# Memory attention of the first layer: second scores with keys on partitions, exponentials as the moving operand

## The chip, the cores and the metric

The kernel runs on one core of a Trainium2 chip. The metric is the device time of one execution in microseconds; the time before is the median of three runs. TensorE is called PE here, VectorE DVE, ScalarE ACT, GpSimd POOL and SyncE SP; PEld is PE's weight load.

## The reference, cut to what matters

The model has four layers with an attention part and a feed-forward part each, on h of 4 x 576 x 64 (64 patch tokens and 512 text tokens in each of 4 batches). The change touches one part, the feed-forward part of layer 0, a memory layer that ends in a causal attention over 8 heads:

```python
q = (x @ Wq).reshape(b, n, HEADS, DIM) * DIM ** (-0.5)      # b=4, n=576, HEADS=8, DIM=64
kv_scores, indices = _pk(x, Wq_pk, pk_keys)
ind = indices + offsets[None, None, :, None]
k = jnp.einsum('bnhk,bnhkd->bnhd', kv_scores, keys_table[ind])
v = jnp.einsum('bnhk,bnhkd->bnhd', kv_scores, values_table[ind])
sim = jnp.einsum('bihd,bjhd->bhij', q, k)
sim = jnp.where(causal, sim, neg)
attn = jax.nn.softmax(sim, axis=-1)
out = jnp.einsum('bhij,bjhd->bhid', attn, v)
out = out.transpose(0, 2, 1, 3).reshape(b, n, HEADS * DIM)
return out @ Wo
```

## The kernel before

The kernel is a row of stages; each opens its own semaphores and a block in which every engine runs its own instruction list, and the next block starts when all are through. `retrieval_stage` (L1508) first makes keys and values with `dense_rows_stage` and writes them to device memory as `kept`, one array of 128 rows (64 of key, 64 of value) by tokens for each head. Then comes the attention, which is what the change replaces. It has 32 heads in all (4 batches by 8 heads), unrolled, with the batch outside. n counts them.

A head has 576 tokens: chunks c = 0 to 4 of 128 queries (the last has 64), chunk c seeing keys 0 to 128(c+1). For each head, `RetrievedAttention` and its parent `CausalAttention` do this:

- SP fetches 128 x 576 of `kept` (L1025), two buffers.
- PE multiplies w_q by xnT to q, 64 x 576 (L1033), and transposes the value rows, five tiles (L1037). DVE copies q with the factor 0.125 (L1045) and v (L1049, L1051) out of PSUM. The same PSUM bank 0 is used in two turns, first q of 512 tokens, then the rest.
- `pe_score` (L811, L813): q chunk as weights, keys as the moving operand; the scores lie in PSUM with queries on partitions.
- `dve_head` (L913): one operation adds the mask, writes the scores to `probs` and takes the row maximum; L916 negates it. ACT takes the exponential with the maximum as bias and the sum as by-product (L881).
- `pe_turn_probs` (L823): 15 transposes of the exponentials to keys on partitions; ACT copies them to `pT` (L871, L874).
- `pe_weigh` (L1061): for chunk c, c+1 products with the turned exponentials (128 x 128) as weights and v (64 columns) as the moving operand.
- `dve_norm` (L893, L896): reciprocal of the row sums, one number for each query, at most 128 x 4; then the product into O.

The order on PE is written out by hand in `pe_head` (L846): the scores of chunks 2 to 4, the turns of q and v of the next head and the first two scores of the next head stand between the transposes and the products of this head. After each batch `project` (L1544, L1552) transposes O, ACT copies it, and PE multiplies by w_o; DVE adds to h (L1588).

All float32 products are written as one call and stand in the trace as two instructions. bfloat16 products and transposes stand as one.

Of the kernel before, what the change touches and what calls it, by code (L numbers as in the profile page):

```python
# [42 lines left out]
class Steps:  # L43
# [3 lines left out]
    def __init__(self, engine, semaphore):  # L47
        self.engine, self.semaphore, self.before, self.count = engine, semaphore, 0, 0
# [639 lines left out]
                nc.gpsimd.memset(ap, value)  # L688


class CausalAttention:


# [306 lines left out]
STRIPS = ((0, 1, 16), (1, 1, 8), (2, 1, 5), (3, 1, 4), (4, 1, 3), (5, 3, 2), (8, 8, 1))  # L1000
PAIRED = sum(n * w for _, n, w in STRIPS)
STRIP_AT = [sum(n * w for _, n, w in STRIPS[:i]) for i in range(len(STRIPS))]


class RetrievedAttention(CausalAttention):

    def __init__(self, nc, core, st, w_q, kept):  # L1010
        super().__init__(nc, core, st, D, 1.0, fetches=None)
        self.w_q, self.kept = w_q, kept
        self.kv = st.sb("kv", [P, 2, SEQ])
        self.kT = self.kv[:, :, :]
        self.qT = st.sb("qT_padded", [P, 2, SEQ])

    def begin(self):
        super().begin()
        set_stage(self.nc, "peer_q_padding", [(self.qT[D:P, :, :], 0.0)])

    def sp_fetch(self, sp, n):
        b, h = n // HEADS, n % HEADS
        if n >= 2:
            sp.wait_ge(self.scored, self.BEGIN + CH * (n - 1))
        sp.dma_start(self.kv[:, n % 2, :], self.kept[h, :, b * SEQ:(b + 1) * SEQ]).then_inc(self.fetched[n % 2], 16)  # L1025

    def pe_turn(self, pe, m, u, tail):
        nc, ps, n = self.nc, self.core.psum, 2 * m + u
        b, h = n // HEADS, n % HEADS
        pe.wait_ge(self.fetched[u], 16 * (m + 1))  # L1030
        pe.wait_ge(self.qk_copied, self.BEGIN + 4 * n + (1 if tail else 0))
        lo, hi = (BANK, SEQ) if tail else (0, BANK)
        last = nc.tensor.matmul(ps[0:D, 0, 0:hi - lo], self.w_q[:, h * D:(h + 1) * D],  # L1033
                                self.core.xnT[:, b * PAD + lo:b * PAD + hi], start=True, stop=True)
        if tail:
            for c in range(CH):
                last = nc.tensor.transpose(ps[0:self.rows[c], 0, (c + 1) * D:(c + 2) * D],  # L1037
                                           self.kv[D:P, u, c * P:c * P + self.rows[c]], self.core.ident[D:P, D:P])
        last.then_inc(self.turned, 1)

    def dve_turn(self, dve, n, u, tail):
        nc, ps = self.nc, self.core.psum
        lo, hi = (BANK, SEQ) if tail else (0, BANK)
        dve.wait_ge(self.turned, self.BEGIN + 2 * n + (2 if tail else 1))
        nc.vector.tensor_scalar(self.qT[0:D, u, lo:hi], ps[0:D, 0, 0:hi - lo], 0.125, None, ALU.mult  # L1045
                                ).then_inc(self.qk_copied, 1)
        if tail:
            dve.wait_ge(self.weighed, self.BEGIN + CH * (n - 1))
            nc.vector.tensor_copy(self.v1[:, u, 0:CH - 1, :], ps[:, 0, D:CH * D].rearrange("p (c d) -> p c d", d=D)  # L1049
                                  ).then_inc(self.qk_copied, 1)  # L1050
            nc.vector.tensor_copy(self.v1[0:TAIL, u, CH - 1, :], ps[0:TAIL, 0, CH * D:(CH + 1) * D]  # L1051
                                  ).then_inc(self.qk_copied, 1)

    def pe_weigh(self, pe, m, u, c):
        nc, ps, d, r, n = self.nc, self.core.psum, self.d, self.rows[c], 2 * m + u
        if c == 0:
            pe.wait_ge(self.normed, self.BEGIN + 2 * n)
        pe.wait_ge(self.p_copied, self.BEGIN + CH * n + c + 1)
        for m in range(c + 1):
            k = self.rows[m]  # L1060
            last = nc.tensor.matmul(ps[0:r, 1, c * d:(c + 1) * d], self.pT[0:k, self.pT_at[c] + m * r:self.pT_at[c] + (m + 1) * r],  # L1061
                                    self.v1[0:k, u, m, :], start=(m == 0), stop=(m == c))
        last.then_inc(self.weighed, 1)


def dense_rows_stage(nc, core, I, norm, kept):
# [438 lines left out]
LOG_AT = ONEHOTS_AT + 2 * HEADS + 2  # L1505


def retrieval_stage(nc, core, I, norm):  # L1508


# [2 lines left out]
    with Stage(nc, "peer") as st:  # L1513
# [3 lines left out]
        kept = nc.dram_tensor("peer_kept", (HEADS, P, TOKENS), F32, kind="Internal").ap()  # L1517
        dense_rows_stage(nc, core, I, norm, kept)
        loads.arrive()
        O = st.sb("O", [P, T, HEADS * D])  # L1520
        o1 = st.sb("o1", [P, 2, HEADS * D])
        set_stage(nc, "peer_padding", [(O[TAIL:P, CH - 1::CH, :], 0.0)])
        A = RetrievedAttention(nc, core, st, w_q, kept)
        A.begin()
        o_turned, o_copied, o_projected, o_added, vec = (
            st.sem(n) for n in ("o_turned", "o_copied", "o_projected", "o_added", "vector_steps"))
        ps = core.psum
        TERMS = HEADS * D // P
        out_of = lambda b, h: (lambda lo, hi, r: O[0:r, b * CH + lo:b * CH + hi, h * D:(h + 1) * D])
        with nc.Block() as block:  # L1530
            @block.sync
            def _(sp):
                for n in range(B * HEADS):
                    A.sp_fetch(sp, n)

            @block.tensor
            def _(pe):
                def project(b):
                    pe.wait_ge(A.normed, A.BEGIN + 2 * HEADS * (b + 1))
                    for t in range(b * CH, (b + 1) * CH):  # L1540
                        if t >= 2:
                            pe.wait_ge(o_copied, t - 1)
                        for k in range(TERMS):
                            last = nc.tensor.transpose(ps[:, 6 + t % 2, k * P:(k + 1) * P], O[:, t, k * P:(k + 1) * P],  # L1544
                                                       core.ident[:, :])
                        last.then_inc(o_turned, 1)
                        for done in ([t - 1] if t % CH else []) + ([t] if t % CH == CH - 1 else []):
                            pe.wait_ge(o_copied, done + 1)
                            if done >= 2:
                                pe.wait_ge(o_added, done - 1)  # L1550
                            for k in range(TERMS):
                                last = nc.tensor.matmul(ps[:, 4 + done % 2, 0:D], o1[:, done % 2, k * P:(k + 1) * P], w_o[:, k, :],  # L1552
                                                        start=(k == 0), stop=(k == TERMS - 1))
                            last.then_inc(o_projected, 1)
                    pe.wait_ge(o_added, (b + 1) * CH)

                for b in range(B):
                    A.pe_start(pe, b * PAIRS, 0)
                    if b:
                        project(b - 1)  # L1560
                    for h in range(HEADS):
                        A.pe_head(pe, b * PAIRS + h // 2, h % 2, h < HEADS - 1)
                project(B - 1)

            @block.scalar
            def _(act):
                def copy(b):
                    for t in range(b * CH, (b + 1) * CH):
                        act.wait_ge(o_turned, t + 1)
                        if t >= 2:  # L1570
                            act.wait_ge(o_projected, t - 1)
                        nc.scalar.activation(o1[:, t % 2, :], ps[:, 6 + t % 2, :], ACT.Copy).then_inc(o_copied, 1)

                for b in range(B):
                    if b:
                        copy(b - 1)
                    for h in range(HEADS):
                        A.act_head(act, b * HEADS + h, h % 2)
                copy(B - 1)

            @block.vector
            def _(dve):
                steps = Steps(dve, vec)

                def add(b):
                    for t in range(b * CH, (b + 1) * CH):
                        dve.wait_ge(o_projected, t + 1)
                        nc.vector.tensor_tensor(core.h[:, t, :], core.h[:, t, :], ps[:, 4 + t % 2, 0:D], ALU.add  # L1588
                                                ).then_inc(o_added, 1)

                for b in range(B):
                    A.dve_start(dve, b * HEADS, 0)
                    if b:
                        add(b - 1)
                    for h in range(HEADS):
                        A.dve_head(dve, steps, b * HEADS + h, h % 2, h < HEADS - 1, h > 0, out_of(b, h),
                                   out_of(b, h - 1) if h else None)
                add(B - 1)


CHANNELS = 3 * D
# [4 lines left out]
FREQ = SEQ + 1  # L1606
FCH = (FREQ + P - 1) // P
FREQ_ROWS = [min(P, FREQ - P * k) for k in range(FCH)]
TOKEN_ROWS = [min(P, SEQ - P * c) for c in range(CH)]


def root_stage(nc, core, name, x, sq, stat, scale, eps, ones=None):
# [1337 lines left out]
```

## Time and profile before

| what | value |
|---|---|
| time, median of 3 runs | 4470.99 us (4460.36 to 4479.04) |
| profiled execution, its own time | 4491.15 us |
| its span | 4489.0 us, granted clock 0.863 |
| PE busy | 3640.8 us (81%), 16965 instructions |
| PEld busy | 2172.9 us (48%) |
| DVE busy | 2651.9 us (59%) |
| ACT busy | 1496.4 us (33%) |
| POOL busy | 359.1 us (8%) |

The page divides the span into 40 slices of 112 us. The attention that is changed lies in the 20th to the 24th. "Idle before" is the time in which an engine stood still just ahead of the instructions of a group, with the releaser that ended most of it. A granted clock of 1.00 is 2.4 GHz, 0.50 is 1.2 GHz; a value between them is a mean over a stretch with both.

### The profile page before, as it was taken

To read this page: it belongs to the slowest core of one execution; us is meant where nothing else is said; L and a number is where in the kernel's file an instruction comes from. 1 tells how busy PE (TensorE), PEld (TensorE's weight loads), DVE (VectorE), ACT (ScalarE), POOL (GpSimd) and SP (SyncE) were. 2 spreads that over 40 slices of the span, in tenths; PEclk is the share of its full clock that TensorE was granted. 3 is DMA by queue.
4 is the path that set the end of the run, shared out by engine and by line. 5 is a ranking of instruction groups with operands and counts; after the bars stand their busy time and mean duration, and the time that the engine had idled before them with its cause. 6 is when DMAs were issued, how large, how long until landed. Compare 5 with 4: busy or idle time off the path is not lost. (4 is left out here: it accounts for less than half of the span.)

```text
span 4489.0 us, 57158 instructions
## 1 busy us (share of the span) xinstructions
PE 3640.8 (81%) x16965; PEld 2172.9 (48%) x17110; DVE 2651.9 (59%) x7758; ACT 1496.4 (33%) x2931; POOL 359.1 (8%) x351
## 2 busy tenths in 40 slices
PE   5528889999999999999799868848869372799867
PEld 4325545544454554444466645437747252344354
DVE  3369878777887877555333322144344555899812
ACT  2203444444444444444333330034432133100023
POOL 1000000000000000000000001111000000355500
PEclk8569999999999999999878877975579665899968
DMA  0102334443443444443000020000010002100000
GB/s 7 52 10 76 102 87 102 87 91 86 101 92 83 101 88 91 107 104 71 24 19 20 21 79 0 0 4 1 1 31 0 1 0 54 43 0 0 0 7 5
DMA packets 140950, 207.83 MB, mean 46 GB/s; under 512 B 35104, under 2 KB 119657, under 8 KB 135469
## 3 DMA queue, kind: packets, MB, share of 16 engines
q1 hardware_dynamic: 140717, 205.03, 19.1%
q8 instruction: 108, 1.77, 0.2%
q14 instruction: 125, 1.02, 0.1%
HBM read 115.66 MB, written 10.03 MB: 28 GB/s over the span
## 5 line engine op out<-in xcount | busy, mean ns | idle before, releaser
L1256 PE MATMUL psum<-pk_W,pk_kv 128*128 128x512 f32 (+1 forms) x2560 | 1203.8, 552 | 10.0 <-issue 9.8
L1487 DVE SCALAR_TENSOR_TENSOR pk_W<-psum,pk_E 128x512 f32<-128x512 f32 (+1 forms) x1280 | 810.5, 633 | 440.3 <-ACT pk_E L1354 407.2
L1354 ACT ACTIVATE pk_E<-psum 128x512 f32<-128x512 f32 (+1 forms) x1280 | 708.8, 554 | 1005.0 <-PE psum L1246 1003.1
L1256 PEld LDWEIGHTS psum<-pk_W,pk_kv 128*128 128x128 f32 x2560 | 465.4, 191 | 173.7 <-issue 27.0
L1245 PE MATMUL psum<-pk_stack,pk_spread 128*128 128x512 bf16 (+1 forms) x1171 | 420.4, 359 | 80.0 <-DVE pk_W L1487 53.6
L1246 PE MATMUL psum<-pk_stack,pk_spread 128*128 128x512 bf16 (+1 forms) x1280 | 459.4, 359 | 17.7 <-DMA pk_stack<-pk_marks 9.5
L2480 PE MATMUL psum<-tree_w,tree_x 128*128 128x512 bf16 x1692 | 381.0, 380 | 112.9 <-PEq L120 90.7
L1245 PEld LDWEIGHTS psum<-pk_stack,pk_spread 128*128 128x128 bf16 x1280 | 125.1, 98 | 444.8 <-DVE pk_W L1487 349.4
L2480 PEld LDWEIGHTS psum<-tree_w,tree_x 128*128 (+1 forms) x1728 | 168.2, 99 | 312.0 <-issue 121.3
L2551 DVE COPY_PREDICATED leaf_acc<-leaf_path,psum 128x512 f32<-128x512 uint32 x468 | 310.4, 729 | 5.1 <-PE psum L2480 2.8
L1246 PEld LDWEIGHTS psum<-pk_stack,pk_spread 128*128 128x128 bf16 x1280 | 125.7, 98 | 241.8 <-issue 232.0
L1220 PEld LDWEIGHTS psum<-pk_ranked,pk_onehot 128*128 128x128 bf16 x2304 | 168.3, 149 | 115.4 <-issue 102.8
L1220 PE MATMUL psum<-pk_ranked,pk_onehot 128*128 128x128 bf16 x2304 | 172.1, 230 | 56.9 <-DVE pk_onehot L1445 56.9
L1190 POOL TENSOR_TENSOR pk_parts<-pk_left,pk_parts 128x512 bf16<-128x512 f32 (+1 forms) x40 | 44.0, 1100 | 1814.9 <-ACT pk_parts L1325 1814.9
L1441 DVE TENSOR_TENSOR pk_onehot<-pk_idf,pk_count 128x2048 bf16<-128x2048 bf16 x144 | 175.4, 1218 | 1.2 <-PE psum L1220 0.6
L295 PE MATMUL psum<-ident,xn 128*64 128x128 f32 x160 | 34.2, 407 | 171.7 <-DVEq L269 157.6
L881 ACT ACTIVATE peer_probs<-peer_probs,peer_stat 128x128 f32<-128x128 f32 (+4 forms) x160 | 96.3, 602 | 222.9 <-DVE peer_stat L916 222.7
L811 PE MATMUL psum<-peer_kv,peer_qT_padded 128*128 128x128 f32 (+4 forms) x320 | 163.3, 603 | 5.9 <-DVE peer_v L1051 3.5
L913 DVE CUSTOM_DVE_ANT_0 peer_probs<-psum,peer_mask 128x128 f32<-128x128 f32 (+4 forms) x160 | 85.9, 537 | 116.2 <-PE psum L811 106.2
L1957 PE MATMUL psum<-moe_x,moe_w 128*85 x480 | 113.8, 388 | 43.6 <-PEq L120 42.3
L1061 PE MATMUL psum<-peer_v,peer_pT 128*128 128x64 f32 (+2 forms) x960 | 139.4, 289 | 0.0
L1061 PEld LDWEIGHTS psum<-peer_v,peer_pT 128*128 128x128 f32 (+2 forms) x960 | 123.7, 202 | 20.7 <-issue 15.3
(513 smaller groups left out, 4970.1 us busy)
## 6 DMA issues: line engine op xcount, KB each, us to landing
pk_kv<-in_kv SPq DMA_DIRECT2D x40, 2048.0 KB, 7.8
pk_stack<-pk_parts SPq DMA_DIRECT2D x768, 64.0 KB, 2.5
pk_stack<-pk_marks SPq DMA_DIRECT2D x256, 64.0 KB, 2.6
peer_kv<-peer_kept SPq DMA_DIRECT2D x32, 288.0 KB, 2.8
peer_kept<-pk_made SPq DMA_DIRECT2D x32, 256.0 KB, 2.1
tree_weights_x<-in_tree_w SPq DMA_DIRECT2D x32, 256.0 KB, 4.6
pk_stack<-pk_parts SPq DMA_DIRECT2D x192, 32.0 KB, 2.0
dft_cos<-in_cos SPq DMA_DIRECT2D x1, 2596.5 KB
```

The costliest lines, as they stand in the source:

```text
L811: last = nc.tensor.matmul(ps[0:r, bank, 0:min(w, BANK)], q, self.kT[:, u, 0:min(w, BANK)], start=True, stop=True)
L1061: last = nc.tensor.matmul(ps[0:r, 1, c * d:(c + 1) * d], self.pT[0:k, self.pT_at[c] + m * r:self.pT_at[c] + (m + 1) * r], self.v1[0:k, u, ...
L1220: last = nc.tensor.matmul(ps[:, 6 + h // 4, h % 4 * P:(h % 4 + 1) * P], onehot[:, h % 2, :, :, r], ranked[:, r, :], start=(r == 0), stop=( ...
L1245: nc.tensor.matmul(ps[:, n % 2, 0:N], spread[:, 1, c % 2, :], of, start=True, stop=True)
L1246: nc.tensor.matmul(ps[:, 2 + n % 2, 0:N], spread[:, 0, c % 2, :], of, start=True, stop=True).then_inc(x_made, 1)
L1256: nc.tensor.matmul(ps[:, 4, 0:N], kv[:, k % 2, c, :], W[:, n % 3, 0:N], start=(c == 0), stop=(c == CHUNKS - 1)).then_inc(acc_done, 1)
L1354: nc.scalar.activation(E[:, n % 2, 0:width(k)], ps[:, 2 + n % 2, 0:width(k)], ACT.Exp).then_inc(e_made, 1)
L1441: steps.do(nc.vector.tensor_tensor(onehot[:, h % 2, :, :, :], idf[:, :, h, :].unsqueeze(2).to_broadcast([P, 2, KEYS, TOP]), count64[:, :, ...
L1487: nc.vector.scalar_tensor_tensor(W[:, n % 3, 0:width(k)], ps[:, n % 2, 0:width(k)], TOP + 0.5, E[:, n % 2, 0:width(k)], ALU.is_gt, ALU.mul ...
L1957: last = nc.tensor.matmul(ps[0:HALF, 3 * which + u % 3, :], w[:, lo:lo + HALF], x[:, bass.ds(g * BANK, BANK)], start=(k == 0), stop=(k == 2))
L2480: last = nc.tensor.matmul(ps[:, n % BANKS, :], x[:, bass.ds(t * P, P)], w[:, c * BANK:(c + 1) * BANK], start=(k == 0), stop=(k == len(prod ...
L2551: ins = nc.vector.copy_predicated(acc[:, u, level + 1, :, :], over(mask.bitcast(U32), D), bank)
```

## The change

`RetrievedAttention` and the blocks that used it go; `memory_attention_stage` takes their place, one block for all 32 heads. The scores with queries on partitions are made as before, in the order of chunks 4, 3, 2, 1, 0, but serve only for the maxima (`peak`); the masked scores are written to a scratch tile and not read. The negated maxima are split into two bfloat16 pieces (`piece`), transposed on PE (`turn_peaks`) and copied to a 32-row tile (`copy_peaks`). The scores are made a second time with keys on partitions (`turned_scores`), and a bfloat16 product of a tile of ones with the pieces adds the negated maxima to them, another with the identity adds the mask. ACT's exponential of three full banks goes to `pT`, which is the moving operand of `weigh`; the weights are v (64 columns) beside 64 columns of ones, so that the output has the values on 64 partitions and the sums on the other 64, sides changing with the parity of the head. `norm` takes the reciprocal of the sums as they lie, 64 x 576, and multiplies. The output stays with the head's dimension on partitions (oT), so that `project` needs no transposes. ACT copies q (for two heads at once) and v out of PSUM, where DVE did.

```diff
+def turned_scores(bank_of, k, q, mask16, ident16, ones16=None, shift=None):
+    a, b, c = bank_of
+    def scores(to, keys, queries):
+        yield to, k[:, keys], q[:, queries], True, False
+        if shift is not None:
+            yield to, ones16[:, 0:to.shape[0]], shift[:, queries], False, False
+    def masked(to, at, n):
+        yield to, ident16[:, :], mask16[:, at:at + n], False, True
+    tri = lambda bank, at: masked(bank[:, at:at + P], LEAD, P)
+    return (
+        [*scores(a[:, :], slice(0, P), slice(LEAD, SEQ)), *masked(a[:, 0:P - LEAD], LEAD + LEAD, P - LEAD)],
+        [*scores(b[0:LEAD, 0:LEAD], slice(0, LEAD), slice(0, LEAD)), *scores(b[LEAD:P, 0:LEAD], slice(BANK, SEQ), slice(BANK, SEQ)),
+         *masked(b[:, 0:LEAD], 0, LEAD), *scores(b[:, LEAD:BANK], slice(P, 2 * P), slice(P, SEQ)), *tri(b, LEAD)],
+        [*scores(c[:, 0:SEQ - 2 * P], slice(2 * P, 3 * P), slice(2 * P, SEQ)), *tri(c, 0),
+         *scores(c[:, SEQ - 2 * P:BANK], slice(3 * P, 4 * P), slice(3 * P, SEQ)), *tri(c, SEQ - 2 * P)])
+def weighed_parts(v, p):
+    return ((slice(0, BANK), v[:, 0, :], p[:, 0, :]),
+            (slice(P - LEAD, BANK), v[:, 1, :], p[:, 1, LEAD:BANK]),
+            (slice(2 * P - LEAD, BANK), v[:, 2, :], p[:, 2, 0:SEQ - 2 * P]),
+            (slice(3 * P - LEAD, BANK), v[:, 3, :], p[:, 2, SEQ - 2 * P:BANK]),
+            (slice(4 * P - LEAD, BANK), v[LEAD:P, 4, :], p[LEAD:P, 1, 0:LEAD]))
...
+SCORE_ORDER = (4, 3, 2, 1, 0)
+SCORE_BANKS = (6, 6, 7, 6, 7)
+SCORE_FREE = (0, 1, 1, 2, 3)
...
+            @block.tensor
+            def _(pe):
...
+                def score(n, j):
...
+                    if n >= 1 or j >= 1:
+                        pe.wait_ge(peaked, CH * n + SCORE_FREE[j])
...
+                def weigh(n, some):
+                    parts = weighed_parts(v[:, n % 4, :, :], pT[:, n % 2, :, :])
+                    for i in some:
+                        pe.wait_ge(exped, 3 * n + (1, 2, 3, 3, 2)[i])
+                        if i == 0:
+                            pe.wait_ge(v_copied, 2 * (n + 1))
+                            if n:
+                                pe.wait_ge(normed, 2 * n)
+                        cols, lhsT, rhs = parts[i]
+                        last = nc.tensor.matmul(ps[:, 1, cols], lhsT, rhs, start=(i == 0), stop=(i == 4))
+                        if i == 4:
+                            pe.wait_ge(q_copied, 4 * min((n + 1) // 2 + 2, heads // 2))
+                            last = nc.tensor.matmul(ps[:, 2, 0:LEAD], v[0:LEAD, n % 4, 0, :], pT[0:LEAD, n % 2, 1, 0:LEAD],
+                                                    start=True, stop=True)
+                            last.then_inc(weighed, 1)
...
+                pe.wait_ge(pad_set, 6)
+                make_q(0)
...
+                for n in range(heads):
+                    more = n + 1 < heads
+                    if n:
+                        weigh(n - 1, (0,))
+                    if more:
+                        score(n + 1, 0)
+                    turn_peaks(n)
+                    if n:
+                        weigh(n - 1, (1,))
+                    if more:
+                        score(n + 1, 1)
+                        score(n + 1, 2)
+                    score_turned(n)
+                    if n % 2 == 0 and n + 2 < heads:
+                        make_q(n // 2 + 1)
+                    if n % HEADS == 3 and n >= HEADS:
+                        project(n // HEADS - 1, n + 2)
+                    if more:
+                        score(n + 1, 3)
+                    if n:
+                        weigh(n - 1, (2, 3, 4))
+                    if more:
+                        score(n + 1, 4)
+                    if n + 2 < heads:
...
+                        turn_v(n + 2)
+                weigh(heads - 1, (0, 1, 2, 3, 4))
+                project(B - 1, heads)
...
+            @block.vector
+            def _(dve):
...
+                def norm(n):
+                    b, h = divmod(n, HEADS)
+                    out, sums = side(n), other(n)
+                    to = oT[out, b % 2, h // 2, :]
+                    dve.wait_ge(weighed, n + 1)
...
+                    nc.vector.reciprocal(inverse[out, LEAD:SEQ], ps[sums, 1, :]).then_inc(inverted, 1)
+                    nc.vector.reciprocal(inverse[out, 0:LEAD], ps[sums, 2, 0:LEAD]).then_inc(inverted, 1)
+                    dve.wait_ge(inverted, 2 * (n + 1))
+                    nc.vector.tensor_tensor(to[:, LEAD:SEQ], ps[out, 1, :], inverse[out, LEAD:SEQ], ALU.mult).then_inc(normed, 1)
+                    nc.vector.tensor_tensor(to[:, 0:LEAD], ps[out, 2, 0:LEAD], inverse[out, 0:LEAD], ALU.mult).then_inc(normed, 1)
...
+                for n in range(heads):
+                    more = n + 1 < heads
+                    if more:
+                        peak(n + 1, 0)
+                    copy_peaks(n)
+                    if more:
+                        for j in range(1, CH):
+                            peak(n + 1, j)
+                        piece(n + 1)
+                    if n % HEADS == 3 and n >= HEADS:
+                        add(n // HEADS - 1)
+                    if n:
+                        norm(n - 1)
+                norm(heads - 1)
+                add(B - 1)
```

P is 128, SEQ 576, BANK 512, LEAD 64. The POOL list of the new block makes both masks (`causal_masks`: two memsets and five selects, one after the other) and then fills six tiles: ones16 (128 x 128), qT (128 x 2304), peaks (128 x 1152, bfloat16), pieces (128 x 320, bfloat16), v (128 x 2560) and oT (128 x 5120). PE waits for all of them. Before, POOL filled peer_O, the mask and the lower half of the q tile, in three blocks.

## Rows read from the trace of the kernel before

**Rows 1.** Windows: the attention, and all that follows it.
```profile
core 0: us, PE busy (x) PEld busy (x) DVE busy (x) ACT busy (x) POOL busy (x), PEclk, DMA share, GB/s
2145.39:2634.80 489.41, 433.43 (x2352) 295.04 (x2352) 179.84 (x756) 179.48 (x532) 5.05 (x4) 0.82 0.07 20
2634.80:4489.00 1854.20, 1339.84 (x6326) 878.67 (x6362) 938.87 (x1711) 440.03 (x795) 296.52 (x274) 0.77 0.05 13
```

**Rows 2.** Waits of PE, 2156 to 2640 us: engine line waited for, total, times, longest.
```profile
PE psum L823 <- ACT peer_probs L881: 34.1, 32, 1.2
PE psum L1033 <- DVE peer_qT_padded L1045: 3.5, 4, 0.9
```

**Rows 3.** Windows: stretches of the attention at either clock.
```profile
2179.00:2185.00 6.00, 4.95 (x28) 2.71 (x26) 3.50 (x12) 1.76 (x6) 0.00 (x0) 1.00 0.17 49
2185.50:2195.00 9.50, 9.50 (x39) 6.69 (x37) 1.51 (x8) 2.93 (x10) 0.00 (x0) 0.50 0.00 0
```

**Rows 4.** Timeline: start, us, engine line; float32 pairs at full clock, then eighteen small products.
```profile
2858.20 0.81 PE L1812 MATMUL psum<-dft_y,dft_isin 128*128 128x384 f32 x2
2858.84 0.81 PE L1812 MATMUL psum<-dft_y,dft_icos 128*128 128x384 f32 x2
...
2623.86 1.97 PE L1061 MATMUL psum<-peer_v,peer_pT 128*128 128x64 f32 x18
```

**Rows 5.** Timeline ahead of the attention: two bfloat16 and two float32 instructions a turn.
```profile
2132.85 0.10 PEld L1245 LDWEIGHTS psum<-pk_stack,pk_spread 128*128 128x128 bf16 x1 [0.24 <-DVE pk_W L1487]
...
2134.14 0.10 PEld L1245 LDWEIGHTS psum<-pk_stack,pk_spread 128*128 128x128 bf16 x1 [0.24 <-DVE pk_W L1487]
```

**Rows 6.** Lines by form, DVE: busy us, mean ns; three widths of reciprocal.
```profile
L2346 DVE RECIPROCAL sparse_soft_stat<-sparse_soft_stat 128x8 f32<-128x8 f32 x20 | 4.1, 203 | 0.7
L232 DVE RECIPROCAL norm_stat<-norm_stat 128x20 f32<-128x20 f32 x8 | 2.2, 278 | 2.3 <-ACT norm_stat L282 2.3
...
L580 DVE RECIPROCAL lin_stat<-lin_stat 128x40 f32<-128x40 f32 x1 | 0.4, 403 | 0.0
```

**Rows 7.** Lines by form: other operations out of PSUM, and a peak's readout.
```profile
L2238 DVE TENSOR_TENSOR sparse_kB<-psum,sparse_k_mask 64x512 f32<-64x512 f32 x4 | 2.7, 683 | 13.6 <-PE psum L2196 13.6
L896 DVE TENSOR_TENSOR peer_O<-psum,peer_stat 64x64 f32<-64x64 f32 x32 | 6.6, 205 | 0.0
L801 DVE COPY rot_soft_qT<-psum 96x512 bf16<-96x512 bf16 x16 | 6.7, 421 | 27.0 <-PE psum L785 27.0
L913 DVE CUSTOM_DVE_ANT_0 peer_probs<-psum,peer_mask 64x576 f32<-64x576 f32 x32 | 24.0, 750 | 4.6 <-PE psum L813 3.2 <-issue 0.4
L913 DVE CUSTOM_DVE_ANT_0 peer_probs<-psum,peer_mask 128x128 f32<-128x128 f32 x32 | 9.3, 292 | 2.4 <-PE psum L811 1.1
L913 DVE DVE_READ_ACCUMULATOR2_ANT peer_stat<- 128x1 f32 x128 | 10.2, 80 | 0.0
L1354 ACT ACTIVATE pk_E<-psum 128x512 f32<-128x512 f32 x1024 | 611.0, 597 | 820.5 <-PE psum L1246 820.4
```

**Rows 8.** PE timeline and windows around an idle stretch of PE.
```profile
2926.23 5.98 PE L315 MATMUL psum<-ident,tnn_uv 128*128 128x128 f32 x38 [5.12 <-PEq L155]
...
2911.00:2921.00 10.00, 10.00 (x32) 4.03 (x30) 0.55 (x1) 0.00 (x0) 0.00 (x0) 1.00 0.00 0
2926.50:2929.50 3.00, 3.00 (x16) 3.00 (x15) 0.69 (x1) 1.04 (x2) 0.00 (x0) 0.50 0.06 13
2929.50:2932.00 2.50, 2.50 (x24) 2.50 (x23) 1.78 (x3) 1.34 (x3) 0.00 (x0) 0.98 0.00 0
```

**Rows 9.** Timeline and lines of POOL's fills; the first product of the attention.
```profile
2145.39 1.80 POOL L688 MEMSET peer_O<- 64x2048 f32 x1 [76.75 <-POOLq L162]
2154.35 1.97 PE L1033 MATMUL psum<-xnT,peer_w_q 128*64 128x512 f32 x2 [14.03 <-DMA peer_kv<-peer_kept]
...
L688 POOL MEMSET tnn_out_g<- 128x2560 f32 x1 | 2.2, 2236 | 67.8 <-POOLq L1802 67.8
L759 POOL TENSOR_SCALAR_AFFINE_SELECT peer_mask<-peer_mask 128x1152 f32<-128x1152 f32 x1 | 1.1, 1145 | 0.1
```

**Rows 10.** Windows: the bfloat16 attention of a later layer, which goes by the same class.
```profile
3040.00:3220.00 180.00, 168.69 (x915) 146.07 (x914) 75.67 (x352) 91.44 (x251) 18.05 (x40) 0.50 0.00 0
```

More of the change, by code:

```diff
@@ L688, in _, with causal_masks @@
                 nc.gpsimd.memset(ap, value)
+LEAD = SEQ - BANK
+TOKEN_ROWS = [min(P, SEQ - P * c) for c in range(CH)]
+def causal_masks(nc, pool, steps, mask, turned_mask):
+    steps.do(nc.gpsimd.memset(mask[:, :], 0.0))
+    steps.do(nc.gpsimd.affine_select(out=mask[:, :], in_=mask[:, :], compare_op=ALU.is_ge, fill=NEG,
+                                     base=PAD - P, pattern=[[-1, 2 * PAD - P]], channel_multiplier=1))
+    twin, corner = turned_mask[:, 0:LEAD], turned_mask[:, LEAD:LEAD + P]
+    steps.do(nc.gpsimd.memset(turned_mask[:, :], 0.0))
+    steps.do(nc.gpsimd.affine_select(out=corner, in_=corner, compare_op=ALU.is_ge, fill=NEG,
+                                     base=0, pattern=[[1, P]], channel_multiplier=-1))
+    steps.do(nc.gpsimd.affine_select(out=twin, in_=twin, compare_op=ALU.is_ge, fill=NEG,
+                                     base=0, pattern=[[1, LEAD]], channel_multiplier=-1))
+    steps.do(nc.gpsimd.affine_select(out=twin, in_=twin, compare_op=ALU.is_ge, fill=0.0,
+                                     base=LEAD - 1, pattern=[[0, LEAD]], channel_multiplier=-1))
+    steps.do(nc.gpsimd.affine_select(out=twin, in_=twin, compare_op=ALU.is_ge, fill=NEG,
+                                     base=LEAD, pattern=[[1, LEAD]], channel_multiplier=-1))
@@ L1002 @@
 STRIP_AT = [sum(n * w for _, n, w in STRIPS[:i]) for i in range(len(STRIPS))]
[L1005 to L1063, printed above, removed]
@@ L1519, in retrieval_stage @@
         loads.arrive()
[L1520 to L1598, printed above, removed]
@@ L1601 @@
+        memory_attention_stage(nc, core, w_q, w_o, kept)
 CHANNELS = 3 * D
@@ L1608 @@
 FREQ_ROWS = [min(P, FREQ - P * k) for k in range(FCH)]
-TOKEN_ROWS = [min(P, SEQ - P * c) for c in range(CH)]
 def root_stage(nc, core, name, x, sq, stat, scale, eps, ones=None):
```

185 lines of the change are left out of this document (added).

## Prediction

> **What bounds the kernel now.** I read the windows first, because the page's 81% for PE is a mean over many stages. The attention that changes takes 489.4 us, from POOL's first fill to the last addition; PE is busy for 433 us of it at a mean clock of 0.82, DVE for 180 and ACT for 179 us [rows 1]. PE's waits say the same: what PE waits for longest is the exponential ahead of the transposes, 34.1 us in 32 heads, and next to nothing else [rows 2]. So PE sets the end here, partly at half clock: the reader sees stretches of 6 us at 1.00 and of 9.5 us at 0.50 in turn [rows 3]. Nothing of the next stage starts before this one ends, so what the stage loses or gains goes into the total one to one.
>
> **PE's pace at full clock.** A pair of float32 instructions over 384 columns starts 0.64 us after the one before it [rows 4], 1.667 ns a column. A turn of one such pair over 512 columns (0.853 us) and two bfloat16 products of 512 takes 1.29 us [rows 5], which leaves 0.218 us for each, 0.427 ns a column. Small products with 128 columns of weights come at 1.97 / 18 = 0.109 us an instruction [rows 4].
>
> **PE's work for a head before.** Scores over 1856 columns 3.09; q 576 columns 1.07; 5 + 15 transposes and 30 products by 0.109, 5.45; the projection, 60 small instructions for five chunks, 6.5 us a batch or 0.8 a head. That is 10.4 us, 334 us for 32 heads; clock and gaps make 489 of it.
>
> **PE's work for a head after.**
> The scores for the maxima stay, 3.09. The second scores run over 1600 float32 columns, 2.67, and 0.22 more because two pairs of 64 columns are bound by the small product's 0.109; the ones and the masks add 1600 + 512 bfloat16 columns, 0.90: together 3.79. The weighing runs over 1600 columns with two small pairs, 2.89. q for two heads at once, half of 1.07, is 0.54. v's turns, 6 by 0.109, are 0.65. The five turned maxima, bfloat16 and 128 columns, lie between 0.055 and 0.109 each; I take 0.3 together. The sum is 11.26 us. The projection falls to 40 small instructions, 4.4 us a batch. So the 30 small products and 15 transposes go, but what comes costs more: PE's own work grows by 0.5 us a head (11.26 + 0.55 against 10.4). All that the change could win is clock and gaps.
>
> **The wait that it adds.** `weigh(n, 0)` waits for `normed` of head n-1, since both use PSUM bank 1. On DVE that `norm` stands behind `peak(n+1, 4)` and `piece(n+1)`, and the score for this peak is issued behind the last product of `weigh(n-1)`. Between them PE has only `turn_v`, 0.65 us. So each head has a chain with no cover: PE's list up to that score, then DVE's tail, then PE again. Behind the waiting product stand all the scores of the next head, and so DVE's peaks and ACT's exponentials.
>
> PE's part is 11.26 - 0.65 = 10.6, with 0.2 for the last product's way into PSUM and 0.2 for the copies of q on ACT that the last product waits for in every other head (four copies of some 0.4 us behind the 0.54 us of scores and the products): 11.0 us.
>
> DVE's part: the 128-wide peak 0.29 and its readout 0.08 [rows 7]; the two small operations of `piece`, with a wait between, 0.4. Then two reciprocals. The rows give 203 ns for 8 numbers a partition, 278 for 20 and 403 for 40 [rows 6]: 6.25 ns a number in both steps, where other operations take 683 ns for 512 and 205 for 64 [rows 7], 1.07 ns. Carried on, 512 numbers take 403 + 472 x 6.25 = 3353 ns and 64 take 553. Before, there were at most 4 a partition. No row is as wide, so the bounds are 0.683 (as cheap as any other operation) and the straight line; 8, 20 and 40 lie on the line to a nanosecond and the direction of the data does not change the operation, so I take the line. The multiplications are 0.683 + 0.205 [rows 7]. `norm` is 4.8 us, hand-overs 0.2. DVE's part is 0.8 + 4.8 + 0.2 = 5.8 us. A head takes 11.0 + 5.8 = 16.8 us at full clock.
>
> The page "VectorE: DVE Perf Modes" of the Trainium skill (section on the lane's hardware ahead of Mode 1x) tells why a reciprocal is slow: it is an iterated division "with a repeat count of 8". Eight cycles of 0.96 GHz would be 8.33 ns a number against the 6.25 that the rows show. By it, with the same fixed part, the reciprocals would take 1.1 + 0.1 us more and the time would be 4654.
>
> **The clock.** PE then stands idle for 5.8 - 0.65 = 5.1 us in every head. The trace has such a gap: after 5.12 us PE comes back at 0.50, in dense work, and has 1.00 some 3.3 us later, from 2926.2 to 2929.6 [rows 8]. 3.3 us at half clock do the work of 1.65 us, so I add 1.65: 18.45 us a head. Bounds: none if the clock doesn't fall (16.8), and twice the stretch (20.1), as in the 9.5 us at 0.50 of [rows 3], where PE's instructions were small.
>
> **The rest.** The exponentials (three by 0.6 us [rows 7]) and the copies of q and v are off the chain but for the 0.2. `copy_peaks` (some 0.45 us by the 421 ns of a 512-wide bfloat16 copy [rows 7]) and the other four peaks (0.75 us the widest [rows 7]) lie under PE's list: the score behind the first peak comes after the turned maxima and a product of 0.75 us. If that cover went, it would cost 0.1 to 0.5 us a head. ACT's freed copies of the probabilities and DVE's of q and v are worth nothing on this chain.
>
> POOL's fills stand ahead of the first product. At 0.87 ns a column (2236 ns for 2560 [rows 9]) the six fills, the two masks' memsets and the selects (1.15 us for the wide one, four of some 0.3) sum to 14.7 us, from 2145.4 to 2160.1; before, PE began at 2154.35 [rows 9]. The bfloat16 fills could be half as long, 0.7 us less. Then at half clock q, ACT's copies, two turns of v, the first scores and peaks take 15 us, and the first pass without weighing 11: the first weighing starts at 2186, 41 us in. Then 30 periods, three projections of 4.4 us and an end of 28 us (last second scores and weighing 7.3, norm and hand-over 5.1, weighing 3.1, norm 4.9, projection and addition 5.2, clock 2.4).
>
> **Sum.** 41 + 30 x 18.45 + 13 + 28 = 635.5 us against 489.4: +146. The profiled execution took 4491.15 us, so 4637 by its own time. It lies 20 us above the median of 4471; the change is laid on the median, 4617 us. With 16.8 us a head it is 4568, with 20.1 it is 4667.
>
> **The rivals.**
> *PE remains the bound (faster).* If `norm` were short, the wait would go under PE's list. The place is the same: `weigh(n, 0)` on `normed`. The period is 11.0 + 1.0 + norm, and the stage breaks even near 13.8 us, that is at a norm of 1.8 us. With reciprocals of 0.683 and 0.205 the norm is just 1.8: no change, 4471, if the clock holds over an idle of 2.1 us. Fully covered, 11.5 us a head, the stage takes 41 + 345 + 13 + 22 = 421 and the time is 4403. For it: PE does run denser, in large products, and the share at half clock would shrink. Against it: the 6.25 ns.
> *The clock stays at half.* In the other attention PE is busy for 169 of 180 us and the clock is 0.50 throughout [rows 10]. If the idle of each head did that here, PE's 10.6 us would be 21.2, a head 27.4 and the time 4886. Against it: [rows 8] shows the rise after just such a gap, and the products here are 512 wide.
> *The change doesn't shorten PE's work at all* is what I forecast already; should PE's large products run below the pace of [rows 4, 5], the other end opens.
>
> "TensorE: Matmul & The Clock Gate" (Back-to-back issue gap) of the Trainium skill gives 131 ns for a product of 512 columns in a stream. The rows have 218 ns, so the trace disagrees. By it PE's part would shrink to 0.6, a head to some 14.2 us and the time to about 4490.
>
> **Chances.** Forecast with its bounds 0.75; reciprocals at eight cycles 0.08; clock at half throughout 0.05; same by cheap reciprocals 0.03, or by the page's pace 0.01; faster because the wait is covered 0.05; slower still by something unseen 0.03. Faster by over 0.5% (22 us, about what a measurement of this kernel tells from no change) 0.05, within it 0.04, slower 0.91. The range, with 10 to 20 us for the start on either side, is 4550 to 4690.
>
> **What would show it.** Right: two RECIPROCALs a head near 3.35 and 0.55 us; PE's longest wait is the weighing on `norm`, about 5 us x 31; a period of 17 to 20 us with some 3 us at 0.50; DVE busy for over 280 us in the stage; first product 6 us later. Wrong: a reciprocal of 512 under 1 us, or a period under 14 us.

## The result, and the profile after

The changed kernel takes 4681.85 us (median of 4, 4679.02 to 4685.61) against 4470.85: ratio 1.0461, 95% interval 1.0433 to 1.0489. It is 211 us slower, inside the range of 4550 to 4690 and 65 us above the forecast of 4617.

The profiled execution has a span of 4683.7 us, 194.7 more than before. The stage accounts for 187.2 of them: from POOL's first fill at 2143.73 to the next stage's first load at 2820.32 it takes 676.6 us against 489.4 [rows 1]. Ahead of it the two differ by 1.7 us. What follows takes 1863.4 us here and 1854.2 before; in the eight experiments below it lies between 1847.0 and 1857.7 with the same code. So I take these 9 us for scatter between executions; no run shows what they are, and 1863.4 is the longest of the ten.

Windows of the changed kernel, with the columns of [rows 1] (length, then busy time of PE, PEld, DVE, ACT and POOL, granted clock, DMA): the stage, and then one head in three pieces: the idle stretch, the stretch at half clock, the rest.

```profile
2143.73:2820.32 676.59, 497.36 (x2080) 269.61 (x2080) 260.40 (x549) 99.78 (x226) 13.41 (x13) 0.81 0.05 14
2419.20:2424.10 4.90, 0.02 (x1) 0.00 (x0) 4.74 (x5) 0.60 (x2) 0.00 (x0) 0.85 0.00 0
2424.20:2429.20 5.00, 5.00 (x12) 1.87 (x13) 0.85 (x3) 0.00 (x0) 0.00 (x0) 0.50 0.00 0
2429.60:2438.00 8.40, 8.40 (x45) 5.00 (x43) 1.90 (x7) 1.79 (x3) 0.00 (x0) 1.00 0.14 35
```

PE was busy for 433 of 489 us before; now it is busy for 497 of 677. Of the 187 us that the stage is longer, 64 are busy time and 123 are idle time (179 us against 56), at nearly the same mean clock (0.81 against 0.82). PE's waits in the stage (waiting line, releaser; total, times, longest) name it; this answers to [rows 2].

```profile
PE psum L1623 <- DVE peer_soft_oT L1756: 150.4, 31, 5.6
PE psum L1566 <- POOL peer_soft_oT L1557: 19.5, 1, 19.5
PE psum L1635 <- DVE peer_soft_oT L1756: 4.7, 1, 4.7
PE psum L1576 <- DVE h L1760: 3.6, 3, 1.2
```

L1623 is the product of `weigh`, L1756 the last operation of `norm`: 31 waits, 4.85 us each. The timeline of one head (start, duration, engine, line) shows what they wait for.

```profile
2418.09 0.49 PE L1589 MATMUL psum<-peer_soft_kv,peer_soft_qT 128*128 128x128 f32 x2
2418.51 0.46 PE L1576 MATMUL psum<-ident,peer_soft_kv 64*128 64x64 f32 x4
2418.62 0.29 DVE L1725 CUSTOM_DVE_ANT_0 peer_soft_masked<-psum,peer_soft_mask 128x128 f32<-128x128 f32 x1 [1.45 <-PE psum L1589]
...
2419.37 3.35 DVE L1752 RECIPROCAL peer_soft_inverse<-psum 64x512 f32<-64x512 f32 x1
...
2422.65 0.49 DVE L1753 RECIPROCAL peer_soft_inverse<-psum 64x64 f32<-64x64 f32 x1
2423.17 0.69 DVE L1755 TENSOR_TENSOR peer_soft_oT<-psum,peer_soft_inverse 64x512 f32<-64x512 f32 x1
2423.78 0.22 DVE L1756 TENSOR_TENSOR peer_soft_oT<-psum,peer_soft_inverse 64x64 f32<-64x64 f32 x1
2424.15 1.19 PE L1623 MATMUL psum<-peer_soft_pT,peer_soft_v 128*128 128x512 f32 x1 [4.93 <-DVE peer_soft_oT L1756]
```

This is the chain of the forecast in its order: last score (L1589), last peak (L1725), both reciprocals, both multiplications, the weighing. The lines by form of DVE give all 32 of each; [rows 6] carried on by a straight line had 3353 and 553 ns. The wide one lies on the line; the one of 64 numbers is 64 ns under it.

```profile
L1752 DVE RECIPROCAL peer_soft_inverse<-psum 64x512 f32<-64x512 f32 x32 | 107.3, 3355 | 13.3 <-PE psum L1626 12.3
L1753 DVE RECIPROCAL peer_soft_inverse<-psum 64x64 f32<-64x64 f32 x32 | 15.6, 489 | 0.0
```

### The profile page after: what moved, and what is told of

Its sections match the earlier page's. It is cut to its first block and busy times, and to the rows that moved or that the text cites. A ratio compares the mean times of both kernels' runs of the same rounds, so it can differ in the third digit from the quotient of the medians.

```text
span 4683.7 us, 55961 instructions
## 1 busy us (share of the span) xinstructions
PE 3723.1 (79%) x16838; PEld 2153.0 (46%) x16838; DVE 2732.5 (58%) x7551; ACT 1417.9 (30%) x2625; POOL 367.6 (8%) x360
## 5 line engine op out<-in xcount | busy, mean ns | idle before, releaser
L1240 PE MATMUL psum<-pk_stack,pk_spread 128*128 128x512 bf16 (+1 forms) x1280 | 462.0, 361 | 90.3 <-DVE pk_W L1482 54.2
L1241 PE MATMUL psum<-pk_stack,pk_spread 128*128 128x512 bf16 (+1 forms) x1280 | 459.3, 359 | 0.0
L1725 DVE CUSTOM_DVE_ANT_0 peer_soft_masked<-psum,peer_soft_mask 64x576 f32<-64x576 f32 (+4 forms) x160 | 86.9, 543 | 387.5 <-PE psum L1589 231.8
L1623 PE MATMUL psum<-peer_soft_pT,peer_soft_v 128*128 128x512 f32 (+4 forms) x320 | 150.3, 581 | 150.4 <-DVE peer_soft_oT L1756 150.4
L1709 ACT ACTIVATE peer_soft_pT<-psum 128x512 f32<-128x512 f32 x96 | 57.3, 597 | 451.8 <-PE psum L1611 451.8
L1589 PE MATMUL psum<-peer_soft_kv,peer_soft_qT 128*64 128x512 f32 (+4 forms) x320 | 151.4, 578 | 1.9 <-DVE peer_soft_stat L1725 1.9
L1623 PEld LDWEIGHTS psum<-peer_soft_pT,peer_soft_v 128*128 128x128 f32 (+1 forms) x320 | 63.2, 227 | 171.4 <-issue 162.9
```

The lines of the kernel that those rows point to most:

```text
L1240: nc.tensor.matmul(ps[:, n % 2, 0:N], spread[:, 1, c % 2, :], of, start=True, stop=True)
L1241: nc.tensor.matmul(ps[:, 2 + n % 2, 0:N], spread[:, 0, c % 2, :], of, start=True, stop=True).then_inc(x_made, 1)
L1589: last = nc.tensor.matmul(ps[0:r, SCORE_BANKS[j], 0:min(w, BANK)], q, k[:, 0:min(w, BANK)], start=True, stop=True)
L1623: last = nc.tensor.matmul(ps[:, 1, cols], lhsT, rhs, start=(i == 0), stop=(i == 4))
```

## The experiments

Theory A is the forecast's: each head is a chain in which DVE's norm lies bare. Its rivals: B, PE's added products are the cost; A', only the wait on the PSUM bank matters, not the order on DVE. C and D are about the clock: C takes the half clock behind each idle stretch for a cost of its own, D for none. The "stage" of a run is the time in its profiled execution from POOL's first instruction to the next stage's first load.

**Copies for the reciprocals.**
```diff
-nc.vector.reciprocal(inverse[out, LEAD:SEQ], ps[sums, 1, :]).then_inc(inverted, 1)
-nc.vector.reciprocal(inverse[out, 0:LEAD], ps[sums, 2, 0:LEAD]).then_inc(inverted, 1)
+nc.vector.tensor_copy(inverse[out, LEAD:SEQ], ps[sums, 1, :]).then_inc(inverted, 1)
+nc.vector.tensor_copy(inverse[out, 0:LEAD], ps[sums, 2, 0:LEAD]).then_inc(inverted, 1)
```


> The two reciprocals of norm are replaced by plain copies of the same shapes; the sums are not inverted, the rest is as in the changed kernel. Theory A (each head is a chain: weigh waits for the norm of the head before, and the reciprocals lie bare in it): the reciprocals of 3.355 and 0.489 us become some 0.69 and 0.21, so a head is 2.95 us shorter, 31 heads 91 us, and the time is 4590; if PE's idle of 2 us instead of 4.9 no longer lets the clock fall, up to 2.4 us a head more, 4517. Theory B (PE's added products, second scores, ones and masks, are what costs): PE's list is unchanged, the time stays within 10 us of 4682.

4546.7 us (ratio to before 1.0169, interval 1.0146 to 1.0193), 135 us below the changed kernel; stage 549.5, 127 us below. The kernel leaves out the inversion of the sums. PE's wait on the norm and the copies, from the waits and the lines by form:

```profile
PE psum L1623 <- DVE peer_soft_oT L1756: 59.3, 31, 2.6
```
```profile
L1752 DVE COPY peer_soft_inverse<-psum 64x512 f32<-64x512 f32 x32 | 22.0, 688 | 13.6 <-PE psum L1626 12.6
L1753 DVE COPY peer_soft_inverse<-psum 64x64 f32<-64x64 f32 x32 | 6.8, 213 | 0.0
```

The wait falls by the 91.1 us expected (150.4 to 59.3). The other 36 us of the stage are clock: in the first 8 us behind each start of a weighing PE is at half clock for 2.7 us in the mean of 31, against 4.9 in the changed kernel, and half of that difference, 31 times, is 34 us. B is out as an account of these 127 us: PE's list was untouched.

**ACT lifts the outputs and sums out of PSUM.**
```diff
+def lift(n):
+    act.wait_ge(weighed, n + 1)
+    if n >= 2:
+        act.wait_ge(normed, 2 * (n - 1))
+    nc.scalar.activation(raw[:, n % 2, LEAD:SEQ], ps[:, 1, :], ACT.Copy).then_inc(lifted, 1)
+    nc.scalar.activation(raw[:, n % 2, 0:LEAD], ps[:, 2, 0:LEAD], ACT.Copy).then_inc(lifted, 1)
...
-pe.wait_ge(normed, 2 * n)
+pe.wait_ge(lifted, 2 * n)
```
The wait changed is that of `weigh(n, 0)`; `norm(n)` waits for `lifted` and reads `raw` in place of PSUM.

> ACT copies the weighed outputs and sums (128x512 and 128x64) from PSUM to SBUF as soon as they are made; weigh of the next head waits for this copy and norm reads the copy. DVE's order is unchanged. Theory A: the wait on norm goes, but on DVE the first peak of the next head still stands behind norm, and the second score waits for that peak; PE then stalls some 2.9 us a head there, a head takes about 14.2 us at full clock instead of 19.7, 30 heads 165 us, time 4515 (4500 to 4560 with half clock after the stall). Theory A' (only the PSUM wait matters): a head falls to PE's own 11.6 us, time 4440. Theory B: within 10 us of 4682.

4547.5 us (1.0173, 1.0151 to 1.0195); stage 546.8. The timeline shows where the wait went:

```profile
2256.40 3.35 DVE L1764 RECIPROCAL peer_soft_inverse<-peer_soft_raw 64x512 f32<-64x512 f32 x1
...
2260.94 0.74 DVE L1737 CUSTOM_DVE_ANT_0 peer_soft_masked<-psum,peer_soft_mask 64x576 f32<-64x576 f32 x1
...
2261.75 1.77 PE L1591 MATMUL psum<-peer_soft_kv,peer_soft_qT 128*128 128x512 f32 x4 [1.92 <-DVE peer_soft_stat L1737]
```

The weighing no longer waits for norm, but the first peak of the next head stands behind norm, and the second score waits for that peak. A' is out: with the bank free a head still takes 15.3 to 15.8 us in most periods. That is more than the 14.2 expected, though the stall at the second score is shorter (54.6 us in 29 waits, 1.9 each, against 2.9). PE's list, 12.4 us by the third experiment and not 11.3, makes 14.3 with that stall; most of the rest is the clock, at 0.50 for 3.4 us in 13 of the 31 periods.

**The same, and norm later on DVE.**
```diff
                     if more:
-                        for j in range(1, CH):
+                        for j in (1, 2):
+                            peak(n + 1, j)
+                    if n >= 2:
+                        norm(n - 2)
+                    if more:
+                        for j in (3, 4):
                             peak(n + 1, j)
                         piece(n + 1)
...
-                    if n:
-                        norm(n - 1)
+                norm(heads - 2)
                 norm(heads - 1)
```


> As the kernel with ACT's copies, and on DVE norm of head n-2 is placed between the third and the fourth peak of head n+1, under PE's second scores. Theory A: no wait on DVE is left bare, PE sets the period at its own 11.26 + 0.3 us a head at full clock; 30 x (19.7 - 11.6) = 243 us less, time 4439, that is 32 us below the kernel before the change; granted clock near 1.00 inside the heads. If the clock falls all the same, up to 4500. Theory B (PE's added products make it slower than before): time stays above 4471.

4460.0 us in 10 runs (0.9967, 0.9954 to 0.998), stage 460.5. Windows of the stage and of four heads in it:

```profile
2142.00:2602.00 460.00, 428.82 (x2080) 248.32 (x2080) 259.55 (x548) 122.12 (x289) 12.87 (x13) 0.95 0.07 21
2231.97:2281.72 49.75, 49.75 (x242) 27.96 (x240) 32.24 (x68) 15.22 (x36) 0.00 (x0) 1.00 0.09 25
```

PE is busy throughout, at full clock, and 49.75 us for four heads is PE's own list: 12.44 us a head. The same products, reciprocals and maxima as in the changed kernel take 222 us less with 64 more copies on ACT. B falls: with all its added products the new form is at the old one's time, a little below. The time is 21 us above the expected 4439; PE's list, 12.44 us where 11.6 were expected, makes 25 us over 30 heads.

**Products in the gap.**
```diff
                         turn_v(n + 2)
+                        if n:
+                            pe.wait_ge(v_copied, 2 * (n + 3))
+                            for _ in range(16):
+                                nc.tensor.matmul(ps[:, 0, :], ident16[:, :], peaks[:, n % 2, 0:BANK], start=True, stop=True)
```


> The changed kernel with 16 bfloat16 products of 512 columns whose output nobody reads, put into PE's idle time behind turn_v (once ACT has copied v): 16 x 0.218 = 3.5 us of the 4.9 us gap. The dependencies on the chain are unchanged. Theory C (each gap lets the clock fall and the half clock costs some 2.4 us a head): the clock stays at 1.00 and the time falls by up to 30 x 2.4 = 73 us, to about 4610. Theory D (the half clock of PE after a gap costs nothing because DVE is late anyway): time within 10 us of 4682, or higher by what the products take.

4615.8 us (1.0326, 1.0304 to 1.0348), stage 615.5: 61 us less with 464 products more. Timeline of the end of the gap, and the window of the head behind it:

```profile
2265.11 3.63 PE L1676 MATMUL psum<-peer_soft_peaks,peer_soft_ident 128*128 128x512 bf16 x16 [0.72 <-ACT peer_soft_v L1699]
...
2269.31 1.10 PE L1623 MATMUL psum<-peer_soft_pT,peer_soft_v 128*128 128x512 f32 x2 [0.57 <-DVE peer_soft_oT L1760]
```
```profile
2269.40:2283.00 13.60, 13.05 (x62) 7.29 (x62) 3.88 (x14) 3.69 (x9) 0.00 (x0) 1.00 0.08 22
```

The wait on norm is still there, merely filled, and the clock stays at 1.00 behind it in the 29 heads that have the products. So C holds and D falls: the half clock behind each gap costs 2.1 us a head (61 us over 29 heads).

**Shorter fills.** This one starts from the third experiment's kernel.
```diff
-nc.gpsimd.memset(peaks[:, :, :], 0.0).then_inc(pad_set, 1)
-nc.gpsimd.memset(v[:, :, :, :], 1.0).then_inc(pad_set, 1)
+nc.vector.memset(peaks[:, :, :], 0.0).then_inc(pad_set, 1)
+nc.vector.memset(v[:, :, :, :], 1.0).then_inc(pad_set, 1)
-nc.gpsimd.memset(oT[:, :, :, :], 0.0).then_inc(pad_set, 1)
+nc.gpsimd.memset(oT[:, :, :, SEQ:PAD], 0.0).then_inc(pad_set, 1)
+make_q(0)
 pe.wait_ge(mask_cast, 2)
 pe.wait_ge(pad_set, 6)
-make_q(0)
```


> The kernel with ACT's copies and the later norm (4460), and the fills cut: DVE fills v and peaks beside POOL, of oT only the padding columns are filled (64 of each 640), and the first product for q goes ahead of the wait for the fills. In the changed kernel POOL's fills end at 2158.0 and q is made at 2160.5; here POOL has 7.7 us of work instead of 14.3, q is in PSUM by then, so ACT's copy of q starts some 9 us earlier: 4451. If DMA or barriers hold the start instead, 4460.

4446.6 us in 6 runs (0.9948, 0.9929 to 0.9967), stage 449.3: the fastest of all, 13 us below the third experiment's 4460.0 (11 us in the stage) where 9 were expected. The changed kernel and this one, first copy of q (timelines):

```profile
2160.62 0.59 ACT L1685 ACTIVATE peer_soft_qT<-psum 64x512 f32<-64x512 f32 x1 [12.27 <-PE psum L1566]
```
```profile
2148.82 0.59 ACT L1685 ACTIVATE peer_soft_qT<-psum 64x512 f32<-64x512 f32 x1 [2.68 <-POOL peer_soft_oT L1557]
```

Counted from POOL's first fill (2143.73 and 2141.51) that is 16.9 and 7.3 us: 9.6 us sooner. POOL, not the loads, had held the start.

**The order, with the weighing still waiting for norm.** ACT lifts only the 64 columns that share bank 2 with the turned maxima, so that a small part of the outputs is freed here too; the 512 columns in bank 1 are not. `weigh` still waits for norm, and its first two parts now stand on PE behind the second scores. On DVE `norm(n - 2)` stands between the third and the fourth of the five peaks, as in the third experiment.
```diff
-                    if n:
-                        weigh(n - 1, (0,))
...
-                    if n:
-                        weigh(n - 1, (1,))
...
+                    if n:
+                        weigh(n - 1, (0, 1))
                     if more:
                         score(n + 1, 3)
```


> The changed kernel with order alone turned: on PE the first two products of weigh stand behind the second scores, on DVE norm of head n-2 stands between the third and fourth peak of head n+1. ACT copies only the 64 columns that share PSUM bank 2; weigh still waits for norm. Theory A: the reciprocals lie under the second scores but for 1.5 us, another 0.7 us is a wait of the second score on the first peak; a head takes 13.5 us against 19.7, time 4496, up to 4560 if the clock falls in these waits. Theory A' (only freeing the bank helps, order does not): no better than 4547, the time with ACT's copies alone.

4504.8 us (1.0079, 1.0054 to 1.0104), stage 506.1, 14.0 us a head where 13.5 were expected. The weighing waits for norm 36.1 us in all where it waited 150.4, and 1.7 us in the head of the timeline:

```profile
PE psum L1627 <- DVE peer_soft_oT L1767: 36.1, 27, 5.1
```
```profile
2245.87 1.85 PE L1627 MATMUL psum<-peer_soft_pT,peer_soft_v 128*128 128x512 f32 x4 [1.69 <-DVE peer_soft_oT L1767]
```

The order on the two engines, with the small copy that it needs, brings 177 us back, more than freeing the bank (134). The freed bank together with the order on DVE alone brings 222. All three together were not run.

**Without ones and mask.** The second scores go without the maxima and without the mask, so the exponentials are of the bare scores, and no key is hidden.
```diff
-        yield to, k[:, keys], q[:, queries], True, False
-        if shift is not None:
-            yield to, ones16[:, 0:to.shape[0]], shift[:, queries], False, False
+        yield to, k[:, keys], q[:, queries], True, True
...
-        yield to, ident16[:, :], mask16[:, at:at + n], False, True
```

> The changed kernel without the bfloat16 products (2112 columns a head: ones by maxima, identity by mask); the exponentials are of the bare scores. Theory A: PE's list is part of the chain, so 2112 x 0.427 ns = 0.90 us a head goes, 29 us in all: 4653. Rival (these products lie beside DVE's norm): no change, 4682. Theory B (they and the second scores are the main cost): 29 us would be most of what the change lost, and the kernel would be near 4471 to 4500.

4644.7 us (1.039, 1.0363 to 1.0416), 37 us less than the changed kernel against 29 expected; stage 642.6, 34 us less. The wait on norm is as long as before:

```profile
PE psum L1622 <- DVE peer_soft_oT L1755: 150.5, 31, 5.6
```

So PE's list is on the chain, and these products are a sixth of the loss. What the second scores themselves cost was not taken out by any run; the third experiment has them whole and still ends at the old time.

**The best order with copies for the reciprocals.**

> The kernel with ACT's copies and the later norm (4460), with the reciprocals replaced by plain copies; the sums are not inverted. Theory A: the reciprocals are covered there, so taking 2.95 us a head from DVE changes nothing: within 10 us of 4460. Rival (a reciprocal hurts wherever it stands, DVE being loaded for 9 of 13 us): 20 to 90 us less.

4455.2 us in 10 runs (0.9964, 0.9949 to 0.998) against 4460.0 (0.9967): 5 us less, within the 10 expected. The profiled executions' stages are 452.3 and 460.5 us, and 6.4 of these 8 us lie behind the start of the last weighing, where no scores are left to cover a norm. The third experiment and this one, last weighing and last projection:

```profile
2583.05 2.96 PE L1625 MATMUL psum<-peer_soft_pT,peer_soft_v 128*128 128x512 f32 x9 [0.90 <-ACT peer_soft_raw L1704]
2592.33 8.80 PE L1637 MATMUL psum<-peer_w_o,peer_soft_oT 128*128 128x64 f32 x40 [6.20 <-DVE peer_soft_oT L1768]
```
```profile
2582.06 2.96 PE L1625 MATMUL psum<-peer_soft_pT,peer_soft_v 128*128 128x512 f32 x9 [0.90 <-ACT peer_soft_raw L1704]
2587.37 6.40 PE L1637 MATMUL psum<-peer_w_o,peer_soft_oT 128*128 128x64 f32 x40 [2.23 <-DVE peer_soft_oT L1768]
```

Between the heads the edit changes nothing: but for those at a projection the periods are 11.8 and 13.1 us in turn in both. What was worth 135 us in the changed kernel is worth nothing where norm lies under PE's list, and 4 us with 2.4 of clock where it lies bare at the end.

## Why the prediction was right, and where its sizes were off

*Direction, place and mechanism* held: the chain, its order, the releaser of the wait and the idle of about 5 us were as forecast, and taking out the reciprocals, the bank's wait or the order (135, 134 and 177 us) each moved the time the way the chain says. Of the signs that the prediction named, the two reciprocals, the wait, the period and the first product (5.5 us later) came as said. The half clock was 4.9 us a head, not some 3, and DVE was busy for 260 us in the stage, not for over 280; for that last figure the prediction shows no sum.

*The size* is less good: +146 us were forecast and +211 measured. The time lies inside the range by 8 us only. The range had been drawn for the length of the half clock and for the start, and what filled it was in the main something else: PE's pace, the end and scatter. That they did not sum to more is in part luck.

*The reciprocals* were forecast as 3353 and 553 ns and measured 3355 and 489. The straight line from three rows of 8 to 40 numbers held at 512 and was 13% high at 64.

*The start* was 41 us to the first weighing: measured 40.8 (2143.73 to 2184.49). *The end* was 28 us and took 34.4 (2785.88 to 2820.32). The last weighing (granted clock 0.56 in its first 4.6 us) and the projection (8.8 us for 40 products, 0.50) ran at or near half clock behind the two last norms; the sum had 3.1 and 4.4 us for them and 2.4 for the clock.

*The period* was 18.45 us and measures 19.7 once norms are in it (584.6 us from 2201.26 to 2785.88, less 13 us of projections, in 29 periods). Three terms were off, by +1.2, -0.6 and +0.8 us (+0.4 by the experiment that fills the gap); together that is 1.0 to 1.4:

- PE's list, 11.26 forecast, 12.44 measured in the third experiment, where nothing else holds PE. The mis-sized step is "PE's pace at full clock" taken for a whole head. The rows of dense streams don't hold where kind, operands or width change from product to product. The timeline of the third experiment has them, start to start:

```profile
2306.60 1.12 PE L1625 MATMUL psum<-peer_soft_pT,peer_soft_v 128*128 128x512 f32 x2
2307.66 1.07 PE L1591 MATMUL psum<-peer_soft_kv,peer_soft_qT 128*64 128x512 f32 x2
...
2308.77 0.53 PE L1601 MATMUL psum<-peer_soft_ident,peer_soft_pieces 128*32 128x128 bf16 x5
...
2313.12 1.00 PE L1613 MATMUL psum<-peer_soft_qT,peer_soft_kv 128*128 128x448 f32 x2
2313.96 0.35 PE L1613 MATMUL psum<-peer_soft_peaks,peer_soft_ones 128*128 128x448 bf16 x1
```

  The 512-column pair of the weighing takes 1.06 us (priced 0.853), the first score of 576 columns 1.11 (0.96), the second scores' pair of 448 columns 0.84 (0.75). Why was not measured.
- The bare wait, 5.5 forecast with its hand-overs and the copies of q, 4.9 measured. The small reciprocal was 0.06 us shorter, and no weighing waits for a copy of q in the trace, for which 0.2 stood in the sum. The rest was not taken apart.
- The clock, 1.65 forecast, 2.45 in the records (4.9 us at 0.50 in the mean of 31 heads, 3.2 to 6.3) and 2.1 by the experiment that fills the gap. The mis-sized step is reading one gap's 3.3 us [rows 8] as the length for all; the range had twice that as its bound.

30 periods by 1.25 and 6 us at the end are 44 us; the stage was 41 us over its forecast of 635.5. The rest of the 65 us is not the stage: 9 us more of the profiled span lie behind it and 2 less ahead of it, and the profiled execution before stood 20 us above its median where the one after stands 4 above its own.

*The rivals.* That PE's period could cover norm was put at 1.8 us of norm for break-even. With copies in place of the reciprocals norm is 1.8 us, and the time is 4547, not 4471. The same two terms are what that estimate lacked: PE's list (1.2 us a head) and the clock behind an idle of 2 us (2.7 us at half, so 1.3 a head). The clock did not stay at half.

Read as eight cycles for each number, the repeat count of 8 that the Trainium skill's page "VectorE: DVE Perf Modes" (section on the lane's hardware ahead of Mode 1x) gives the division would have made the wide reciprocal 4.4 us, by an estimate from that page. The trace disagrees, with 3.355.

## What to carry to other kernels

When a layout is turned, count what becomes wide: reciprocals of at most 4 numbers a partition became ones of 512 and 64, at 6.25 ns a number against 1.07 for a multiplication. Then ask what stands between the last producer and the first consumer of the shared buffer, on each engine's own list: here moving the norm behind three maxima of a later head on DVE, and the start of the weighing behind the second scores on PE, was worth 177 us, while leaving out the products of ones and masks was worth 37. Price PE's list from a stretch with the same mix of products, not from a row of equal ones.

## What the runs showed of the hardware

The reciprocal's time lies on a straight line for 8, 20, 40 and 512 numbers a partition: 203, 278, 403, 3355 ns. The one of 64 numbers, right behind the wide one, took 489 ns, 64 under the line. Idle of 4.9 us is followed by 3.2 to 6.3 us at half clock in dense work; idle of 2 us by none in 10 of 31 heads and by 3.0 to 6.6 us in the others (the first experiment). Filling 3.6 us of the idle with 16 products that nobody reads made the changed kernel 66 us faster, though the weighing still waits for the same norm.
